# A graph network kernel: the first aggregation takes 30 of 104 edge groups as dense block products, and a block's tile is added by two engines

## The reference

```python
def reference(x, src, dst, ...):
    # network 0 (GIN): one aggregation, two matmuls
    agg = segment_sum(x[src], dst)
    h1 = (agg + x) @ W1 + b1                       # 256 -> 1024
    h1 = relu(batchnorm(h1) * gamma + beta)        # mean and variance over all nodes
    x = layernorm(x + relu(h1 @ W2 + b2))          # 1024 -> 256
    # network 1 (GCN): three aggregations, norm = dinv[src] * dinv[dst], loops added
    h = x
    for W, b in ((W1, b1), (W2, b2), (W3, b3)):
        h = relu(segment_sum((h @ W.T)[src] * norm, dst) + b)
    return layernorm(x + h)
```

## Time and profile before

| | us |
|---|---|
| median of 3 runs | 2933.99 (2928.63 to 2935.6) |
| profiled execution, its own span | 2930.2 |
| first tile multiplied in pass 0 | 74.9 |
| last gather of pass 0 issued | 1088.0 |
| last hidden matmul of pass 0 ends | 1109.95 |
| first gather of pass 1 | 1312.0 |

### The profile page before, as it was taken

The page is one execution under the profiler, slowest core; times in us unless marked ns, Lnnn a source line. Parts: engine busy times, 40 slices in busy tenths (PEclk is TensorE's granted clock), DMA queues, the critical chain, the costliest instruction groups (busy, mean ns, idle before and its releaser), DMA issues.

```text
span 2930.2 us, 44233 instructions
## 1 busy us (share of the span) xinstructions
PE 2390.3 (82%) x15784; PEld 1770.1 (60%) x15784; DVE 1427.8 (49%) x3556; ACT 956.0 (33%) x1512; POOL 2020.2 (69%) x2141
## 2 busy tenths in 40 slices
PE   3676666766666678999999987899998889999986
PEld 2444444444444447776777765677776667777754
DVE  7787777678677775760223233122222321424234
ACT  0111111111111115554444433444444334344431
POOL 6777777777777760017777777677777757777774
PEclk9988878888878888999999999999999999999998
DMA  4444554555454446987889898779898977888894
GB/s 136 141 159 143 162 161 141 161 160 161 143 160 159 144 148 219 344 305 251 296 297 308 285 330 297 242 255 307 298 311 297 312 235 245 298 275 285 272 315 127
DMA packets 360951, 680.17 MB, mean 232 GB/s; under 512 B 44051, under 2 KB 190441, under 8 KB 354827
## 3 DMA queue, kind: packets, MB, share of 16 engines
q0 software_dynamic: 102576, 295.31, 32.3%
q10 hardware_dynamic: 154688, 222.02, 22.6%
q1 hardware_dynamic: 103451, 159.81, 15.4%
HBM read 559.42 MB, written 117.51 MB: 231 GB/s over the span
## 4 chain that ended last, share of the span: by engine, by line
PE 60%; DVE 17%; DMA 9%; issue 7%; DVEq 2%; ACT 2%; POOL 0%; SPq 0%; ACTq 0%; POOLq 0%
PE ps L1074 30%; PE ps L938 8%; PE ps L976 6%; PE ps L920 6%; DVE vreg L1263 5%; PE ps L986 4%; DMA hbuf<-parts_d 4%; DMA xs<-in_x_dram 3%; PE ps L950 2%; DVEq L1220 2%; DVE vreg L1250 1%; DVE vreg L1244 1%; PE ps L963 1%; DMA xs<-x_d 1%; ACT strips L679 1%
## 5 line engine op out<-in xcount | busy, mean ns | idle before, releaser
L632 POOL DMA_INDIRECT ring<-table_d,idx x1236 | 1183.6, 958 | 437.7 <-issue 375.4
L1074 PE MATMUL ps<-wide,hbuf 128*128 128x512 f32 x4116 | 1039.7, 404 | 38.0 <-DMA hbuf<-parts_d 32.1
L632 POOL DMA_INDIRECT ring<-in_x_dram,idx x832 | 821.0, 987 | 264.0 <-issue 251.6
L1074 PEld LDWEIGHTS ps<-wide,hbuf 128*128 128x128 f32 x4116 | 760.4, 191 | 262.5 <-issue 60.7
L792 ACT CAST wide<-abuf 128x1024 fp32r<-128x1024 uint8 (+1 forms) x588 | 552.5, 940 | 633.3 <-PE ps L1074 632.6
L1216 DVE TENSOR_TENSOR acc<-acc,ps 128x256 f32 x260 | 107.5, 413 | 663.8 <-PE ps L938 662.5
L920 PE MATMUL ps<-ring,hot 128*32 128x256 f32 x4136 | 317.4, 429 | 101.1 <-issue 82.7
L950 PE MATMUL ps<-vreg 128*128 128x300 bf16 x840 | 197.3, 345 | 231.0 <-DVE vreg L1263 212.2
L938 PE MATMUL ps<-place,strips 128*128 128x128 f32 x2068 | 317.9, 303 | 64.7 <-ACT strips L679 34.6
L938 PEld LDWEIGHTS ps<-place,strips 128*128 128x128 f32 x2068 | 295.1, 214 | 105.9 <-ACT strips L679 55.8
L1263 DVE TENSOR_TENSOR vreg<-vreg,ps 128x600 f32 x420 | 329.4, 784 | 54.4 <-DVE vreg L1263 23.6
(11 more groups left out here) (131 smaller groups left out, 1541.2 us busy)
## 6 DMA issues: line engine op xcount, KB each, us to landing
hbuf<-parts_d ACTq DMA_DIRECT2D x84, 1024.0 KB
hbuf<-parts_d ACTq DMA_DIRECT2D x84, 768.0 KB
abuf<-ad_d ACTq DMA_DIRECT2D x63, 896.0 KB
parts_d<-vreg SPq DMA_DIRECT2D x72, 512.0 KB, 7.2
h_d<-ureg SPq DMA_DIRECT2D x23, 1024.0 KB, 7.3
ureg<-h_d POOLq DMA_DIRECT2D x23, 1024.0 KB, 8.2
ad_d<-vreg SPq DMA_DIRECT2D x28, 784.0 KB, 4.2
ring<-table_d,idx POOLq DMA_INDIRECT x1236, 4.9
```

Source lines behind the costliest of these rows:

```text
L632: pool.indirect_dma_start(out=ring[:, i % SLOTS, j, :], out_offset=None, in_=table[0:N, :], in_offset=at).then_inc(g["rows"][i % SLOTS], 16)
L1074: ins = pe.matmul(ps[:, 2 + 4 * q + h, 0:(n1 - 4 * q) * P].rearrange("p (s n) -> p s n", n=P), hbuf[:, bl, e * D + h * P:e * D + (h + 1) * P],
```

## The change

**Two dense runs in pass 0.** The first two runs of `DENSE` (30 groups, 240 tiles, 16 supergroups) are not gathered in pass 0. Their tiles are built first, between item 2 and item 36 of the 74 groups that are left (seven tiles an item), the other 180 tiles after them (five an item). From item 12 on, `dense_step0` multiplies the stored blocks in four half runs of four supergroups, 49 steps each, 196 steps of four matmuls of 512 columns. For this the source table has to stand in `parts[1]` in an upper and a lower part: `make_part` does that for the 25 chunks of `x` in items 1 to 9 (SP loads 256 KB, DVE makes the two parts with two instructions, SP stores 512 KB; two buffers, each of which is free again when its store has landed). SP loads a row of 256 KB for each step, three steps ahead (`load_row`), and 448 KB of blocks for every seven steps (`load_quad`); ACT widens the bytes (`widen0`); DVE adds each half run to `acc` (`add_quad`). The edges of the 30 groups are still counted, by "light" groups (`light_strips`, `keep_counts`, `light_sums`, `add_counts`).

**A tile's addition.** PE has one pair of banks left for tiles, the other holds the dense sums. DVE adds only the first of the 12 destination columns of a tile (50 numbers), ACT copies the other 11 (550 numbers), since they are still zero in the block. The next tile's matmuls wait for both (`s_ba`, `s_bc`). There are two `ablk`, cleared by ACT (`clear_block`) instead of DVE. Of the one-hots, `lohot` is made for two tiles at once.

**Buffers and order.** `ring` has 3 slots in pass 0; its fourth holds `split0`. `hs` has one half for all chunks but one, so a chunk's copies wait until the chunk before is stored. One list, `PLAN`, gives the order of all engines. Chunks retire in the order 4, 5, 11, 0, 12, 13, 14, 1, ...

```diff
+HALFRUNS = 4
+QUAD = 4
+SLOTS0 = 3
...
+    PARTS_AT = [list(range(3 * s - 3, min(3 * s, NCH + 1))) if HALFRUNS and s else [] for s in range(NS0)]
...
+    for s in range(NS0):
+        steps = iter(STEPS0[s])
...
+        work = [("strips", s, 0)] + [("own", TURN0[c], 0) for c in AT0[s][:1]] + one_step() + [("sums", s, 0)]
+        work += [("lstrips", s, 0)] * len(LIGHT_AT[s]) + one_step() + [("lsums", s, 0)] * len(LIGHT_AT[s])
...
+            for pr in range(HP):
+                work += [("hidden", TURN0[c], pr)] + one_step()
+        work += [("dense", k, 0) for k in steps]
+        more = [("part", c, 0) for c in PARTS_AT[s]] + [("tile", t, 0) for t in TILES_AT[s]]
+        behind = [[] for _ in work]
+        for n, m in enumerate(more):
+            behind[(2 * n + 1) * len(work) // (2 * len(more))].append(m)
...
-        TB = 6
+        TB = 4
...
-        BUILDBANK = (2, 6)
+        BUILDBANK = 2
...
             def store_block(g):
                 sp.wait_ge(s_ba, LAST[g] + 1)
+                sp.wait_ge(s_bc, LAST[g] + 1)
...
+            def load_part(c):
+                u = c % 2
+                wait(sp, s_part, 2 * (c - 1))
+                sp.dma_start(tile_of(xparts, u, c), rows_of(x, c)).then_inc(s_partl[u], 16)
...
+            def load_row(k):
+                b = k % NB
+                wait(sp, s_step0, k - QUAD + 1)
+                sp.dma_start(hbuf0[:, k % QUAD, :].bitcast(F32), parts[1][b * P:(b + 1) * P, :]).then_inc(s_row[k % QUAD], 16)
...
+            gather(0, x, SPARSE0)
...
+            def clear_block(g):
+                wait(act, s_bst, (g - 1) * 16)
+                act.copy(aclear[g % 2], zeros[:, 0:1].to_broadcast([P, NBP * P // 4])).then_inc(s_bz, 1)
...
+                act.wait_ge(s_ba, t + 1)
+                wait(act, s_bc, t)
+                act.copy(ablk[g % 2][:, :, bass.ds(starts[t % READ] + 1, SPAN - 1)].rearrange("p (e b) n -> p e b n", e=2),
+                         tile_bank(SPAN)[:, :, :, 1:SPAN]).then_inc(s_bc, 1)
...
             def build(t):
                 pe.wait_ge(s_oh, t + 1)
-                wait(pe, s_ba, t - 1)
+                wait(pe, s_ba, t)
+                wait(pe, s_bc, t)
...
+            def dense_step0(k):
+                j, b = k // NB, k % NB
+                pe.wait_ge(s_row[k % QUAD], (k // QUAD + 1) * 16)
+                pe.wait_ge(s_wide0, k + 1)
...
             def tile_hot(t):
                 at, j = t // TILES, t % TILES
-                wait(dve, s_bm, t - TB + 1)
-                dve.tensor_scalar(lohot[:, t % TB, :], iotal, lot[:, at, j:j + 1], None, ALU.is_equal)
+                wait(dve, s_bm, t - TB + 2 - t % 2)
+                if t % 2 == 0:
+                    dve.tensor_tensor(lohot[:, t % TB:t % TB + 2, :], lot[:, at, j:j + 2].unsqueeze(2).to_broadcast([P, 2, P]),
+                                      iotal.unsqueeze(1).to_broadcast([P, 2, P]), ALU.is_equal)
                 dve.tensor_scalar(jhot[:, t % TB, :], iotaj, keyt[:, at, j:j + 1], None, ALU.is_equal).then_inc(s_oh, 1)
...
-                tile = ps[:, BUILDBANK[t % 2]:BUILDBANK[t % 2] + 2, 0:JW // 2].rearrange("p e (b n) -> p e b n", n=SPAN)
-                dve.tensor_tensor(to, to, tile, ALU.add).then_inc(s_ba, 1)
...
+                wait(dve, s_bc, t)
+                to = ablk[g % 2][:, :, bass.ds(starts[t % READ], 1)].rearrange("p (e b) n -> p e b n", e=2)
+                dve.tensor_tensor(to, to, tile_bank(SPAN)[:, :, :, 0:1], ALU.add).then_inc(s_ba, 1)
+
+            def make_part(c):
...
+                q, nb = slice(0, min(size(c), P)), len(blocks(size(c)))
+                dve.wait_ge(s_partl[u], 16 * (c // 2 + 1))
+                wait(dve, s_partst[u], 16 * (c // 2))
+                t, upper, rest = xparts[q, u, 0:nb, :], split0[q, u, 0:nb, 0, :], split0[q, u, 0:nb, 1, :]
+                step(dve.tensor_scalar(upper.bitcast(I32), t.bitcast(I32), UPPER, None, ALU.bitwise_and))
+                dve.tensor_tensor(rest, t, upper, ALU.subtract).then_inc(s_part, 1)
```

More of the change, by code:

```diff
@@ new lines, in gnn_kernel, with one_step @@
+    assert not HALFRUNS or (sum(PARTS_AT, []) == list(range(NCH + 1)) and not any(PARTS_AT[READY0 - 1:]))
+    PLAN = []
+    for s in range(NS0):
+        steps = iter(STEPS0[s])
+        def one_step():
+            return [("dense", k, 0) for k in itertools.islice(steps, 1)]
+        work = [("strips", s, 0)] + [("own", TURN0[c], 0) for c in AT0[s][:1]] + one_step() + [("sums", s, 0)]
+        work += [("lstrips", s, 0)] * len(LIGHT_AT[s]) + one_step() + [("lsums", s, 0)] * len(LIGHT_AT[s])
+        for c in AT0[s]:
+            if c != AT0[s][0]:
+                work.append(("own", TURN0[c], 0))
+            for pr in range(HP):
[5 more added lines that the diff above has]
+            behind[(2 * n + 1) * len(work) // (2 * len(more))].append(m)
+        PLAN.append([x for w, ms in zip(work, behind) for x in (w, *ms)])
@@ new lines, in keep_tile @@
+            def keep_tile(t, starts):
+                g = max(g for g in range(NS) if FIRST[g] <= t)
+                if t == FIRST[g]:
+                    act.wait_ge(s_bz, g + 1)
+                if t == 0:
+                    act.wait_ge(s_pad, 32)
+                if t % READ == 0:
+                    n = min(READ, NT - t)
+                    _, starts[:] = nc.values_load_multi_w_load_instructions(
+                        offs[0:1, t:t + n], [mybir.EngineType.Activation], min_val=0, max_val=P - SPAN,
+                        skip_runtime_bounds_check_because="the row is cut to these bounds where it is made")
+                act.wait_ge(s_ba, t + 1)
+                wait(act, s_bc, t)
+                act.copy(ablk[g % 2][:, :, bass.ds(starts[t % READ] + 1, SPAN - 1)].rearrange("p (e b) n -> p e b n", e=2),
+                         tile_bank(SPAN)[:, :, :, 1:SPAN]).then_inc(s_bc, 1)
+                if t == FIRST[g] + SUPER // 2 and g + 1 < NS:
+                    clear_block(g + 1)
@@ L958, in transpose_own @@
                 if a == 0:
[L959 removed]
+                    wait(pe, s["hs"], r * HP)
                 for b, rows in blocks(size(c)):
@@ new lines, in add_quad @@
+            def add_quad(j, n):
+                starts = columns(bases, FIRST0[j], QUAD, N - 1)
+                dve.wait_ge(aggs[0]["acc"], n)
+                dve.wait_ge(s_step0, (j + 1) * NB)
+                for m, g in enumerate([*range(0, QUAD, 2), *range(1, QUAD, 2)]):
+                    if g == 1:
+                        dve.wait_ge(s_dacc0, QUAD * j + m)
+                    to = acc[:, :, bass.ds(starts[g], P)]
+                    dve.tensor_tensor(to, to, ps[:, 6:8, g * P:(g + 1) * P], ALU.add).then_inc(s_dacc0, 1)
+                dve.wait_ge(s_dacc0, QUAD * (j + 1))
@@ L1409, in _ @@
             dve.drain()
[L1410 to L1416 removed]
+            starts, done = [], 0
+            for i, work in enumerate(PLAN):
+                light = LIGHT_AT[i]
+                if i == BEGIN:
+                    flag = regular(dve)
+                    tile_hot(0)
+                    tile_hot(1)
+                for what, n, pr in work:
+                    if what == "strips":
+                        if light:
+                            make_hot(0, LITEM[i], light[0], True)
+                        elif i + 1 < NS0:
+                            make_hot(0, ITEM[i + 1], SPARSE0[i + 1])
+                    if what == "sums":
+                        add_group(0, i, SPARSE0[i])
+                        done = ITEM[i] + 1
+                        if light:
+                            make_hot(0, ITEM[i + 1], SPARSE0[i + 1])
+                    if what == "lsums":
+                        add_counts(i, light[0])
+                        done = LITEM[i] + 1
+                    if what == "part":
+                        make_part(n)
+                    if what == "tile":
+                        if n + 2 < NT:
+                            tile_hot(n + 2)
+                        add_tile(n, starts)
+                    if what == "dense" and n % NB == NB - 1:
+                        add_quad(n // NB, done)
+                    if what == "hidden":
+                        if pr == 0:
+                            hidden_in(fast[0], n, (aggs[0]["acc"], ITEM[i] + 1))
+                        hidden_out(fast[0], n, pr)
+                if i == 0:
                     step = order(dve, s_key)
```

494 lines of the change are left out of this document (308 added, 186 removed).

## The result

| | before | after |
|---|---|---|
| median of 4 runs, us | 2933.4 (2928.6 to 2935.6) | 3054.4 (3045.9 to 3057.2) |
| span of the profiled execution | 2930.2 | 3055.4 |
| last gather of pass 0 starts | 1088.0 | 1182.8 |
| last hidden matmul of pass 0 ends | 1109.95 | 1224.2 |
| first gather of pass 1 | 1312.0 | 1431.2 |

The changed kernel takes 1.041 times as long (95% interval 1.040 to 1.043): 121 us more, where 42 more were forecast. Pass 0 ends 114 us later. Some 5 us more are lost between its end and pass 1 (119 us later there), and passes 1 to 3 take 6 us more in the profiled execution, which is the longest of its four. So the loss is in pass 0, as the prediction had it, and its size is what has to be explained.

What follows compares the result with a forecast made beforehand. Gathers on POOL (1.295 us each) bounded pass 0; tile handovers would follow. Items 274 + 345 + 389 + 113 plus clock 31 gave pass 0 1152 us against 1110, +42, so 2976 us; range 2940 to 3020, eight in ten 2880 to 3055.

Steps and rivals of the forecast that it cites:

- the tile's handover: Pass 0, between tiles: each waits for VectorE's addition, then ScalarE's copy; 1.13 us, in a tile's cycle of 1.55 us.
- clock term: Pass 0 from item 12 on: a tenth of the time at the low clock (0.95 granted), 31 us over 62 items.
- items 37 to 64: Pass 0, five tiles each: 16 without a chunk 170 us, 12 with one 219, together 389 us before the clock.
- VectorE's leg of the handover: Tile's addition in pass 0: 50 numbers from PSUM, taken as 0.21 us from a row of 49 numbers.
- the bound of 1.4: Upper bound of a tile's handover: 1.4 us if strided bytes or register offsets cost a quarter of a microsecond.
- The copy: ScalarE's copy of a tile's 550 numbers from PSUM in pass 0: 0.61 us.
- The hops between engines: Within a tile's handover: TensorE to VectorE 0.21 us, to ScalarE 0.05, back to TensorE 0.05.
- The dense step: Pass 0, four matmuls of 512 columns on TensorE: 1.0 us a step, 196 steps 196 us.
- The parts: Items 0 to 11: each item's third part waits for the first's store, some 5 us eight times; 274 us to item 12.
- The first dense step: Its row load was costed at nothing: 256 KB, 4.5 us to landing, sent three steps ahead.
- The rival by which the clock stays at 0.83: Pass 0: a third of the time at the low clock, 71 us more, 3047 us; chance 0.13.
- The faster rival: Handovers mostly covered, 0.85 us each, below 0.98 to decide: pass 0 ends at 1056, 2880 us; chance 0.27.

Runs made afterwards that it cites:

- both edits: Changed kernel with VectorE adding all 12 columns and parts spread among the tiles: 2934.0 us against 2936.5 for the kernel before, ratio 0.9991.

## Why the prediction was right and wrong

- **Direction and mechanism: right.** The gathers stopped being the bound, and the tile's handover through two engines took their place. The profile has what was named: the last gather is at 1182.8 and not at 778, POOL waits for TensorE (416 us), TensorE waits before L1157 for L856 (267.7 us; forecast some 200). The runs with the split undone show on three chips of 3600 us that the handover is on the path; on a chip of 2936 us the run with both edits takes the whole loss away.
- **Where the 72 us of pass 0 are that were missed.** The copy of an item's counts (L822), once an item, cuts pass 0 up (an item starts some 2.6 us ahead of it); the last column is the version with both edits, on its chip of 2936 us. The forecast's clock term of 31 us is shared out by items.

| stretch | forecast | measured | missed by | with both edits |
|---|---|---|---|---|
| up to the start of item 12 | 274 | 288 | +14 | 246 |
| items 12 to 36 | 357 | 397 | +40 | 350 |
| items 37 to 64 | 403 | 408 | +5 | 387 |
| items 65 to 73 | 118 | 131 | +13 | 121 |

- **The term that failed: VectorE's leg of the handover.** The prediction put it at 0.21 us, from a reading of 49 numbers into a row of numbers, which it called the nearest row, and left the dearer case, strided bytes or register offsets at a quarter of a microsecond more, to the bound of 1.4. It measured 0.38 (379 ns mean over 420), and the whole handover came to 1.38 to 1.54 us for the 1.13 of the forecast. The run with bytes in a row prices the leg at 41 us, on a chip on which the change as a whole costs nothing; on the first chip 0.17 us for each of 248 waits is 42 of the 72, the largest single term, as an estimate. The waits stand 48 up to item 12, 119 in items 12 to 36, 60 in items 37 to 64 and 21 after. The nearest row was near in count and not in form: it writes a row of four-byte numbers, the addition writes single bytes 128 apart.
- **The copy: right alone, short in the kernel.** Forecast 0.61 us, alone 0.619, in the kernel 0.675 in the mean (420 copies, 283.6 us), since 119 start at a dear column. At 248 waits the 0.065 more are 16 us, worked out and not shown by a run of its own. The hops between engines (from the end on one to the start on the next) measured 0.38 together (0.13, 0.10, 0.15), forecast 0.31: by the same count 17 us. The terms come to more than the 72; they overlap other work, and no run tells them all apart.
- **The dense step: right.** Forecast 1.0 us behind a tile, measured 0.92 from the end of the tile's pair to its own.
- **Items 37 to 64: right**, within 5 us, for the reason given: with a chunk's hidden matmuls between the tiles the handovers are covered. The 12 items with a chunk took 227 us (forecast 219, and 6 for the clock), the 16 plain ones 181 (170, and 8). In the version with both edits the 12 are no shorter (234), the 16 are (153).
- **The parts: the total near, the shape not.** VectorE waits for their DMAs 22.9 us in nine waits (forecast eight of some 5), and items 0 to 11 took 14 us more than forecast: items 3 to 5 the 63 us forecast, 6 to 8 69 for 63, 9 to 11 56 for 47. VectorE's two instructions for a part took 0.44 and 0.70 us; the 0.38 and 0.60 of the earlier trace rows are means that mix in a shorter form, which makes 4 us over 25 parts.
- **The first dense step: a wait costed at nothing.** It stands in item 12, and so among the 40 us, and not ahead of it:

```profile
290.15 0.42 PE L1157 MATMUL ps<-vreg 128*128 128x300 bf16 x2 [0.90 <-DVE vreg L1484]
296.97 2.07 PE L1169 MATMUL ps<-wide,hbuf 128*128 128x512 f32 x4 [6.40 <-DMA hbuf<-parts_d]
```

  SyncE's own order made it late: the last part was sent off to be stored at 234.37, but the first row (L674) stands behind the store of a chunk's hidden layer (L600):

```profile
234.37 0.25 SPq L662 DMA_DIRECT2D parts_d<-ring  x1
...
289.51 0.32 SPq L600 DMA_DIRECT2D h_d<-ureg  x1
290.01 0.37 SPq L669 DMA_DIRECT2D quads<-ad_d  x1
290.42 2.54 SPq L674 DMA_DIRECT2D hbuf<-parts_d  x3
```

  The forecast had rows three steps ahead and SP behind no wait that TensorE has not passed; for the first step neither held. The version with both edits pays it too (8.0 us).
- **The clock: near in the middle, low at both ends.** Forecast 0.95 from item 12 on; granted were 0.91 in items 12 to 36 (0.88 up to 500 us), 0.94 in items 37 to 64, and 0.82 after them. At the forecast's own 5 us an item the difference is an estimated 10 us of the +40, 3 of the +5 and 12 of the +13. The rival by which the clock stays at 0.83 came within 7 us of the time, but the clock was 0.93 between 300 and 1150 us: luck.
- **The faster rival fell** with the handover: it needed less than 0.98 us, and even one operation and no split gives 1.06.
- **Passes 1 to 3** were costed at nothing; some 5 us came between the end of pass 0 and pass 1, and 6 behind it in the one execution profiled, both unexplained.

## What to carry over

Splitting an operation between two engines shortens each engine's share and lengthens the chain. Where a buffer is handed round, count the chain: an addition of 0.38 us, a hop of 0.10 and a copy of 0.62 to 0.82 took the place of one operation of 0.78. Price an operand by its form, not only by its count, and take that price from a row, or a run of its own, with the same type, stride and start. An order written as "all of these, then all of those" hides a cost (here 36 us in one set of runs, 9 in another) that a reshuffle of three lines takes away. And where an instruction is long in some places and short in others, see whether the same ones are long in every trace before blaming a neighbour.

## What the runs showed of the hardware

- VectorE: 50 bytes 128 apart 377 ns, 50 four-byte numbers 128 numbers apart 239, in a row 207; 25 of the scattered bytes 266. ScalarE's copy of 550 shows no such difference (619 and 617 ns).
- ScalarE's copy of 50 runs of 11 bytes takes 0.62 to 0.68 us where a run starts 0 to 5 over a multiple of 8, and 0.77 to 0.82 where it starts 6 or 7 over it: all 420 copies, the same in six traces.
- A start address from a register costs VectorE nothing that can be seen (376 against 377 ns).
- Halving a VectorE addition of 600 numbers (786 ns) gives two of 464.
- The same kernel takes 2935 us on some chips and 3600 to 3640 on others, with waits that the profile puts down to no engine of the core; there a change that costs 4.1% on the first costs nothing that can be seen (0.9998 and 1.0013). A verdict belongs to the chip it was made on.
